# A gate computed for two pairs of tiles apart, and rounded copies made by VectorE alone

## The reference, cut to what matters

```python
x = x + gelu(x @ W.T + fc_bias + ((x @ v) / 128 @ u.T) / 16 + cond)      # layer 0
gate_in = concat([mean(all), mean(head+proprio), mean(wrist+proprio)])    # per batch
logits = (gate_in @ gate_w + gate_b) * (1 + scale) + shift                # scale, shift from cond
w_be = top-2 of softmax(logits), renormalized                             # 32 x 4 weights
for e in range(4):
    out += w_be[:, e] * mask[e] * (gelu(x @ ew1[e] + eb1[e]) @ ew2[e] + eb2[e])
x = x + out + gelu(x @ sw1 + sb1) @ sw2 + sb2
```

## Time and profile before

| | |
|---|---|
| median of 3 runs | 241.7 us (241.41 to 241.79) |
| profiled execution | 240.64 us, of which span 238.4 us |
| PE busy | 230.7 us, 97% of the span |
| DVE busy | 200.5 us, 84% |
| ACT busy | 142.6 us, 60% |
| POOL busy | 19.4 us, 8% |
| granted TensorE clock | 1.00 over the whole span |

### The profile page before, as it was taken

One profiled execution on the slowest core, in us unless ns is written; L12 is line 12 of the kernel. 1 busy time (PEld: TensorE's weight loads), 2 busy tenths in 40 slices (PEclk: granted clock), 3 DMA queues, 4 the chain that ended last, 5 costly groups with the idle time before them and its releaser, 6 DMA issues.

```text
span 238.4 us, 3425 instructions
## 1 busy us (share of the span) xinstructions
PE 230.7 (97%) x1194; PEld 197.0 (83%) x1194; DVE 200.5 (84%) x456; ACT 142.6 (60%) x279; POOL 19.4 (8%) x46
## 2 busy tenths in 40 slices
PE   8999988999999999999999999999999999999995
PEld 8887676788788887888888887888888889899894
DVE  0489999999896867976899999995999989778883
ACT  3699998817965097744977079443654075553531
POOL 8000000024000010002000030002000030020000
PEclk9999999999999999999999999999999999999999
DMA  6895000000010000100010000100010000100011
GB/s 174 235 313 135 1 1 0 3 0 0 3 44 0 0 0 4 44 0 1 3 43 1 3 0 1 44 0 3 0 44 0 3 0 1 44 3 1 0 44 44
DMA packets 11256, 7.40 MB, mean 31 GB/s; under 512 B 3776, under 2 KB 10600, under 8 KB 11240
## 3 DMA queue, kind: packets, MB, share of 16 engines
q1 hardware_dynamic: 10760, 7.07, 10.1%
q10 hardware_dynamic: 288, 0.10, 0.2%
q0 software_dynamic: 192, 0.03, 0.1%
HBM read 5.09 MB, written 2.10 MB: 30 GB/s over the span
## 4 chain that ended last, share of the span: by engine, by line
PE 76%; DVE 11%; ACT 10%; issue 2%; POOL 0%; DVEq 0%; ACTq 0%; POOLq 0%
PE ps L522 23%; PE ps L524 22%; PE ps L523 22%; ACT h L428 4%; DVE hs_lo L816 2%; PE ps L528 2%; ACT L428 2%; ACT L409 2%; PE ps L540 2%; PE ps L571 1%; ACT W_raw L414 1%; PE ps L665 1%; DVE segsum L791 1%; PE ps L579 1%; DVE hs_lo L834 1%
## 5 line engine op out<-in xcount | busy, mean ns | idle before, releaser
L428 ACT ACTIVATE h<-ps,b_col 128x512 f32<-128x512 f32 (+1 forms) x160 | 90.5, 639 | 58.8 <-PE ps L524 55.7
L834 DVE SCALAR_TENSOR_TENSOR hs_lo<-h,w_be,hs_hi 128x344 fp32r<-128x344 f32 (+1 forms) x124 | 73.6, 656 | 0.0
L522 PE MATMUL ps<-x_hi,W_hi 128*128 128x512 f32 (+2 forms) x168 | 65.8, 392 | 1.8 <-ACT h L428 0.6
L524 PE MATMUL ps<-x_lo,W_hi 128*128 128x512 f32 (+2 forms) x168 | 60.7, 362 | 0.0
L523 PE MATMUL ps<-x_hi,W_lo 128*128 128x512 f32 (+2 forms) x168 | 60.7, 361 | 0.0
L522 PE MATMUL ps<-hs_hi,W_hi 128*128 128x512 f32 (+1 forms) x156 | 57.3, 367 | 1.1 <-DVE hs_lo L816 0.7
L524 PE MATMUL ps<-hs_lo,W_hi 128*128 128x512 f32 (+1 forms) x156 | 56.9, 365 | 0.0
L523 PE MATMUL ps<-hs_hi,W_lo 128*128 128x512 f32 (+1 forms) x156 | 56.6, 363 | 0.0
L826 DVE TENSOR_SCALAR hs_hi<-h,w_be 128x344 fp32r<-128x344 f32 (+1 forms) x120 | 45.0, 439 | 8.3 <-PE ps L524 4.1
L522 PEld LDWEIGHTS ps<-x_hi,W_hi 128*128 128x128 f32 x168 | 31.7, 189 | 10.6 <-ACT h L428 2.9
L523 PEld LDWEIGHTS ps<-x_hi,W_lo 128*128 128x128 f32 x168 | 31.7, 189 | 4.4 <-issue 1.0
(11 more groups left out here) (121 smaller groups left out, 177.2 us busy)
## 6 DMA issues: line engine op xcount, KB each, us to landing
W_raw<-in_L_cond_ew SPq DMA_DIRECT2D x8, 256.0 KB, 6.4
out<-x_tok SPq DMA_DIRECT2D x7, 256.0 KB, 2.2
x_tok<-in_x SPq DMA_DIRECT2D x3, 512.0 KB, 5.8
x_tok<-in_x SPq DMA_DIRECT2D x2, 256.0 KB, 3.4
W_raw<-in_L_cond_sw SPq DMA_DIRECT2D x2, 256.0 KB, 4.8
out<-x_tok SPq DMA_DIRECT2D x2, 128.0 KB, 1.7
F_pad<-in_fside_Bx1x1024x SPq DMA_DIRECT2D x2, 64.0 KB, 6.1
W_raw<-in_L_cond_W ACTq DMA_DIRECT2D x1, 64.0 KB, 2.9
```

The lines of the kernel that those rows point to most:

```text
L428: ins = nc.scalar.activation(span(h[:, k % 3, c, :], s), up_bank(k, c), ACT.Gelu_apprx_tanh, bias=b1_col[:, s, c:c + 1])
L522: nc.tensor.matmul(dst, w_hi, m_hi, start=start, stop=False)
L524: return nc.tensor.matmul(dst, w_hi, m_lo, start=False, stop=stop)
L834: nc.vector.scalar_tensor_tensor(lo[:, :, c], h[:, k % 3, :, c], w_be[:, t * NB + b, s - 1:s], f32(hi[:, :, c]), ALU.mult, ALU.subtract).t ...
```

## The change

`GATES` splits tiles 0-3 into 0-1 and 2-3. The part for tiles 0-1 is done ahead of the loop, its input before the last tile's residual. The part for 2-3 takes the places inside the loop that the later pairs have. `HALF_HI` = 0: ACT makes no high copy of a shared step, DVE casts all four groups. ACT's tanh stands ahead of gelu(1), PE's logits(0) behind one group of up(1).

```diff
-    GATES = [(0, 4), (4, 6), (6, 8)]
+    GATES = [(0, 2), (2, 4), (4, 6), (6, 8)]
...
-    HALF_HI = 2
+    HALF_HI = 0
...
             gelu(0)
+            gate_tanh(0)
             gelu(1)
-            gate_tanh(0)
...
             up(0)
-            up(1, range(CH // 2))
+            up(1, range(1))
             logits(0)
-            up(1, range(CH // 2, CH))
+            up(1, range(1, CH))
...
-                dve.wait_ge(segsum_ok, NSEG * (g + 3))
+                dve.wait_ge(segsum_ok, NSEG * (g + 2))
...
                     segment_sums(1, 2)
+                    gate_in(0)
                     weight_low(WEIGHTS[3])
-                residual(t)
-                if t == 2:
-                    output_rows()
+                if t < NA - 1:
+                    residual(t)
+            output_rows()
             x1_low(1)
-            segment_sums(2, 4)
-            gate_in(0)
             dve.wait_ge(bias_in, 16 * 3)
             modulation()
-            split(0)
+            residual(NA - 1)
             read_logits(0)
             gate_maximum(0)
             gate_ranks(0)
+            split(0)
+            gate_weights(0)
             split(1)
-            gate_weights(0)
             weight_low(WEIGHTS[4])
             weight_low(WEIGHTS[5])
...
                 if g is not None:
+                    if GATES[g][1] == NA:
+                        segment_sums(*GATES[g])
                     gate_in(g)
```

## The result

| | before | after |
|---|---|---|
| median of 5 runs each | 241.7 us (241.41 to 241.79) | 240.09 us (239.65 to 240.62) |
| profiled execution | 240.64 us, span 238.4 | 239.97 us, span 237.8 |

The ratio is 0.9938, 95% interval 0.9923 to 0.9953: faster by 1.6 us, where 0.79 was forecast, and 240.09 lies 0.2 under the low end of the range. The direction was right and the size was not. The profiled executions differ by only 0.67.

A forecast was written before the change was run, and what follows sets the result against it. PE follows DVE until about 42 us, then itself. Waits and slow restarts worth 1.77 us vanish against a 0.98 us later start, gaining 0.79 at up(5): 241.7 - 0.79 = 240.9 us, 8-in-10 range 240.3 to 241.8.

The forecast's parts named there:

- The chain: DVE's order up to split(2), which PE follows: down(1) 0.98 us later, then 1.77 us of waits and slow restarts gone.
- Prices taken from the late gates: Half-width gate work costs what later instances cost: input 0.46 us, read to ranks 2.48, weights 2.04.
- The tanh ahead of gelu(1): On ACT, waiting for DVE's maximum near 24.9 us; gelu(1) starts near 25.1, cost nothing.
- ACT's copies of split(2): Four rounded copies behind gelu(3), the fourth near 38.2 us; DVE wants it at 38.7, margin 0.5.
- The late pair at 44 to 57 us: Gate work of tiles 2-3 inside the loop: split(5) ends at 57.41, DVE's lead at down(5) falls from 1.35 to 0.43 us.
- E: The forecast case for the whole kernel: gain 0.5 to 1.3 us, chance 0.63.
- Rival A: At down(5), the late half of the gate makes split(5) late; 242.3 us if 2 us late; chance 0.05.
- Rival B: TensorE's clock halves in the new idle ahead of down(0), net 2.0 us lost there, 242.9 us; chance 0.04.
- Rival C: On DVE ahead of down(1), casts cost and half-width ranks and weights save nothing, 1.25 us more: 242.2 us; chance 0.04.
- Rival D: Same mechanism, smaller: down(1) at 36.1 or later, or lead at down(5) short; gain 0 to 0.48, 241.4 us; chance 0.24.
- The advice of the Trainium skill: Offload a saturated DVE to Scalar; by that rule alone the two casts lose 1.22 us, giving 242.9 us.
- the casts' 1.22: One more 128x1024 cast on DVE in each of split(0) and split(1), 0.61 us each, +1.22 by split(1)'s end.

The follow-up runs named there:

- e1: The changed kernel unaltered, timed again beside the kernel before on one chip: 240.34 us, ratio 0.9966.
- e6: The changed kernel unaltered, timed once more in another job beside the kernel before: 240.46 us, ratio 0.9964.
- e15: The changed kernel unaltered, timed a third time beside the kernel before: 240.71 us, ratio 0.9971.
- e5: The changed kernel with 14 instead of 7 filling matmuls ahead of the first transpose: 243.15 us, ratio 1.0069 to the kernel before.
- e0: The kernel before unaltered, timed again beside itself as a null: 241.0 us, ratio 0.9994.
- e12: The kernel before with 40 filling matmuls, then PE waiting for a DVE chain of 8 copies: 249.88 us, ratio 1.0351.
- e13: The changed kernel with 40 filling matmuls, then PE waiting for a DVE chain of 8 copies: 248.95 us, ratio 1.0312 to the kernel before.
- e7: e2 with ACT's high copy of x1 of tile 3 moved behind its late side-matrix copies: 239.3 us, ratio 0.9916 to the kernel before.
- e9: The changed kernel with 26 filling matmuls, then PE waiting for a DVE chain of 7 copies: 255.27 us, ratio 1.0334 to the kernel before.
- e2: The changed kernel with HALF_HI = 2, the gate split alone without the added DVE casts: 239.28 us, ratio 0.9926 to the kernel before.
- e11: The kernel before with gate_weights(0) moved ahead of split(1) at full width: 243.24 us, ratio 1.0072.

## Why the prediction was wrong in size, point by point

**The chain: right, each step within 0.1 us.**

| step | forecast | trace after |
|---|---|---|
| down(0) starts | 30.2 | 30.23 |
| split(1) ends, the remainders start | 35.53 | 35.51 |
| down(1) starts | 35.76 | 35.74 |
| split(2) starts | 36.74 | 36.71 |
| up(4) starts | 38.59 | 38.57 |
| split(2) ends, the remainders start | 39.39 | 39.36 |
| down(2) starts | 40.62 | 40.53 |
| up(5) starts | 43.83 | 43.74 |
| split(5) ends | 57.41 | 57.40 |
| down(5) starts | 57.84 | 57.75 |

Prices taken from the late gates held at the new place. The tanh ahead of gelu(1) cost nothing: gelu(1) at 25.06 for 25.1 forecast. ACT's copies of split(2) end at 35.62 + 2.55 = 38.17, for 38.2, and DVE never waits for them. The late pair at 44 to 57 us fits in; down(5) has no wait.

**The gain: 0.79 forecast, 0.71 to 0.93 measured with the ordinary and the timed start.** 0.89 in e1, 0.82 in e6, 0.71 in e15, 0.93 with the timed start, 0.83 by the distance in the traces; held (e5) there was none. Over all later executions the median of before is 241.31 (68 of them) and of after 240.43 (29): 0.88.

**The step that failed: "the runs' median is 241.7, 1.06 above the profiled execution, so 241.7 - 0.79 = 240.9".** It takes the distance of a kernel's median to its one profiled execution as a constant that the change carries over. For after that distance is 240.09 - 239.97 = 0.12, and for e0, e1, e6 and e15 it is 0.02, -0.24, 0.01 and 0.36. The chain's own sum, 240.64 - 0.79 = 239.85, came within 0.12 of after's profiled 239.97; what went wrong is the carrying over. The distance is mostly the moment at which PE's rate steps up, drawn anew in every execution: in twelve profiles with the ordinary start the first product begins between 6.00 and 7.24, and with the start timed the scatter of over 1 us falls to 0.12 and 0.05 (e12, e13). Before's profiled execution, at 6.26, was an early one. In the first comparison all five runs of before were at 241.41 or above, where 25 of 68 later ones are, and the five of after had 239.65 to 240.62. Some 0.7 us of the 1.6 would then be such a draw. That it is one is inferred, since only one of those ten executions has a profile; whether by chance alone or by something of that chip stays open. The three later medians of after (240.34, 240.46, 240.71) lie inside the range of the prediction. (The range holds all of E, whose 1.3 gives 240.4; "but for its last tenth" is a slip.)

**Rival A** (split(5) late): did not happen in after, whose lead was as worked out; it does in e7, where down(5) comes 0.38 earlier than in after and waits 0.48. **Rival B** (the clock falls in the new idle): given 0.04 as a yes or no; it is neither. It happens in 7 of 34 executions of after, in 8 of 10 of e5 and in one profile (e9). The forecast's price was 2.0 us; the profile has 1.03 at up(5), where the 0.60 of idle ahead of down(1) has taken in a part. The seven lie 0.2 to 0.6 us above their fellows, a difference in which the scatter of the start is left. After's median hardly sees it (240.43 over the 29 later executions, 240.41 over the 23 of them without it), but e5's does: there it is the likely reason that the gain is gone. With the ordinary start it made the change slower in no comparison. **Rival C** (casts cost, half width doesn't pay): its first half is measured (1.19), the second refuted by e2 and by DVE's rows, where ranks and weights took what was forecast. **Rival D** (small errors): they were 0.1 at most. The advice of the Trainium skill (Perfetto Trace Analysis, Optimizing Scalar/DVE Operations) to offload a saturated DVE did not decide the sign, as the prediction had it, but it points at what the change left on the table: 1.06 us, e2.

## What to carry to other kernels

Before a difference under half a per cent is forecast to a tenth of a microsecond, look at what scatters between executions of one kernel; a distance between two events inside the trace repeated to 0.16 us here (while no clock fell) where whole times scatter by 1.6, and a timed start, once its idle was 1.6 us or less, brought the scatter of whole times to a tenth. When two edits come together, run each alone: here one gained 1.95 and the other gave 1.1 of it back, and the better kernel was one constant away. When the engine that is waited for gets more work, the price is paid at the next wait, however idle it is on average: all of the casts' 1.22 on the kernel before, and 0.87 on top of the gate, where without them another engine was last. And a new idle stretch of TensorE can cost a fall of the clock on top of its length: look at the clock of single executions, not only at that of the profiled one.

## What the runs showed of the hardware

TensorE's first matmuls run at 7 in a microsecond and later at 10 to 11, the step comes anywhere from 4 to 7 us after the start of the span, and the granted clock reads 1.00 on both sides of it. Twenty-eight fill matmuls took 4.92 or 6.34 us by that alone. After 3.15 us of idle the granted clock stood at 0.50 for about 3 us of matmuls; behind 1.9 us it stood at 1.00 in the profiles of after and e13, and at 0.59 in that of e9. A fall there cost 1.03 us. The length of the idle alone doesn't decide: at the end of the span, where TensorE has nothing left to do, the clock was at 0.64 in e0's stretch from 237.5 to 238.0 us, behind a last matmul that ended at 236.19, and still at 1.00 at the end of e11, 2.5 us behind the last. (Means of 0.997 to 0.999 in single executions can be this; it costs nothing.) What else decides is not settled.
